# TensorE's two programs change places behind its branch, three long plain float32 products stand in front of the branch, and TensorE's last wait goes

## What is computed

```
gate = x W_gate^T + 0.5 * B_gate[i] (A_gate[i] x)      # i: the entry's own low-rank weights, 16 to choose from
up   = x W_up^T   + 0.5 * B_up[i]   (A_up[i] x)
act  = silu(gate) * up
down = act W_down^T + 0.5 * B_down[i] (A_down[i] act)
m    = max(max|down|, 1e-5) per token
out  = x + (down / m) W_2bit^T * (m * scale) + bias    # W_2bit: four levels, -1.5 to 1.5
```

## Time and profile before

| | us |
|---|---|
| median of 3 runs | 896.11 (895.1 to 896.49) |
| the profiled execution | 895.7 |
| its span in the profile | 894.0 |
| TensorE busy | 877.1 (98% of the span) |
| VectorE, ScalarE, GpSimd busy | 414.6, 275.3, 82.3 |

### The profile page before, as it was taken

How to read it: one execution, slowest core, us unless ns; L and a number is a source line. 1 busy time by engine, 2 the same in 40 slices (tenths; PEclk the granted TensorE clock), 3 DMA queues, 4 the chain that set the end, 5 groups by cost and what they waited for, 6 DMA issues and landing times.

```text
span 894.0 us, 12944 instructions
## 1 busy us (share of the span) xinstructions
PE 877.1 (98%) x3880; PEld 710.1 (79%) x3880; DVE 414.6 (46%) x813; ACT 275.3 (31%) x518; POOL 82.3 (9%) x117
## 2 busy tenths in 40 slices
PE   6999999999999999999999999999999999999996
PEld 6788788888888888888888888888888888878875
DVE  4653467333572236623464234832258223573334
ACT  3642442223421224222333114322242223412113
POOL 1100012010030000300003000030001200020110
PEclk9999999999999999999999999999999999999999
DMA  5532222110201011110111101111111110010011
GB/s 176 150 116 75 91 61 58 49 27 18 63 26 48 23 26 56 38 36 23 38 44 38 36 23 52 39 42 31 28 52 41 39 32 15 14 36 23 23 36 50
DMA packets 43834, 42.33 MB, mean 47 GB/s; under 512 B 12656, under 2 KB 30832, under 8 KB 43808
## 3 DMA queue, kind: packets, MB, share of 16 engines
q1 hardware_dynamic: 41904, 39.16, 15.8%
q10 hardware_dynamic: 1744, 2.56, 0.9%
q0 software_dynamic: 160, 0.33, 0.1%
HBM read 33.62 MB, written 8.39 MB: 47 GB/s over the span
## 4 chain that ended last, share of the span: by engine, by line
PE 94%; DMA 2%; DVE 1%; ACT 1%; issue 1%; SPq 0%; DVEq 0%; ACTq 0%
PE pp_up L1939 26%; PE pp_gate L1939 24%; PE pp_down L2017 23%; PE ps_misc L2073 6%; PE ps_td L2006 4%; PE ps_misc L1939 2%; PE pp_down L2027 2%; PE pp_up L1986 2%; PE pp_gate L1986 2%; DMA rows<-w_gu 2%; PE pp_gate L1929 1%; PE pp_down L2073 1%; ACT wgu L895 0%; DVE actp_full L1551 0%; PE pp_down L2042 0%
## 5 line engine op out<-in xcount | busy, mean ns | idle before, releaser
L2017 PE MATMUL pp_down<-actp_split,wd 128*128 128x512 f32 x960 | 233.3, 392 | 0.0
L1939 PE MATMUL pp_up<-xw,wgu 128*128 128x512 f32 x948 | 229.4, 391 | 0.3 <-DVE actp_full L1551 0.3
L2017 PEld LDWEIGHTS pp_down<-actp_split,wd 128*128 128x128 f32 x960 | 180.3, 188 | 45.1
L1939 PEld LDWEIGHTS pp_up<-xw,wgu 128*128 128x128 f32 x948 | 178.3, 188 | 39.1 <-DVE actp_full L1551 0.7
L1939 PE MATMUL pp_gate<-xw,wgu 128*128 128x512 f32 x864 | 208.0, 390 | 0.9 <-ACT actp_full L1079 0.8
L1551 DVE TENSOR_TENSOR actp_full<-pp_up,actp_full 128x512 f32<-128x512 f32 (+1 forms) x87 | 60.1, 690 | 299.6 <-PE pp_up L1986 278.0
L1939 PEld LDWEIGHTS pp_gate<-xw,wgu 128*128 128x128 f32 x864 | 162.0, 188 | 35.7 <-issue 1.7
L1079 ACT ACTIVATE actp_full<-pp_gate 128x512 f32<-128x512 f32 (+1 forms) x80 | 47.6, 595 | 288.6 <-PE pp_gate L1986 288.6
L1095 ACT ACTIVATE actp_split<-actp_full 128x512 fp32r<-128x512 f32 x80 | 50.6, 632 | 161.4 <-DVE actp_full L1551 157.6
L1047 ACT ACTIVATE bp_split<-b_raw 32x256 fp32r<-32x256 f32 (+1 forms) x176 | 71.2, 405 | 2.4
L1560 DVE TENSOR_TENSOR actp_split<-actp_full,actp_split 128x512 fp32r<-128x512 f32 x80 | 55.4, 692 | 21.2 <-ACT actp_split L1095 20.9
(11 more groups left out here) (135 smaller groups left out, 646.1 us busy)
## 6 DMA issues: line engine op xcount, KB each, us to landing
x_raw<-x_feat SPq DMA_DIRECT2D x118, 64.0 KB, 1.7
rows<-w_gu SPq DMA_DIRECT2D x8, 512.0 KB, 4.4
rows<-x_tok SPq DMA_DIRECT2D x64, 64.0 KB, 1.8
more_rows<-x_tok SPq DMA_DIRECT2D x64, 64.0 KB, 1.8
out<-rows SPq DMA_DIRECT2D x64, 64.0 KB, 1.6
out<-more_rows SPq DMA_DIRECT2D x60, 64.0 KB, 1.6
rows<-w_down SPq DMA_DIRECT2D x9, 256.0 KB, 2.6
b_raw<-b_rows SPq DMA_DIRECT2D x16, 92.0 KB, 2.5
```

The costliest lines, as they stand in the source:

```text
L1939: return nc.tensor.matmul(ps_out[0:m, a:b], w, xw[:, part, k, a:b], start=start, stop=stop)
L2017: last = nc.tensor.matmul(pp_down[:, h, :], wd[0:w, wp, f, h * P:(h + 1) * P], actp_split[0:w, ap, f % 2, :], start=(f == 1 and n == 0), s ...
```

## The change

TensorE alone gets new instructions. Its branch is turned round: "if the flag is 0: general program, else: pair program", so that the general program stands right behind the branch and the pair program behind that one, in front of the end of the block. The flag is loaded ahead of `ps_run` instead of behind it. Between `ps_run` and the branch stand three new products of 128x512 on plain float32 operands (the same bytes as the warm-up's, read as float32). The warm-up has 11 products ahead of the flag where it had 10, and 2 at the head of the pair program where it had 24. The wait for `stored_rows[2]` at the end of the pair program is gone. The other engines run as before.

```diff
-WARM_UP = (10, 24)
+WARM_UP = (11, 2)
+LONG_WARM_UP = 3
...
-                pe.wait_ge(stored_rows[2], 16 * 4 * WIDE_TILES)
-
             pe.wait_ge(columns_ready, 2)
             pe.wait_ge(one_hot_ready, 1)
             nc.tensor.matmul(ps_plan, plan_columns, one_hot, start=True, stop=True).then_inc(plan_gathered, 1)
             warm_up(0)
+            flag = pair_flag(pe)
             pe.wait_ge(run_column_ready, 1)
             nc.tensor.matmul(ps_run, run_column, one_hot, start=True, stop=True).then_inc(run_gathered, 1)
-            flag = pair_flag(pe)
-            with pe.If(flag == 1):
+
+            for _ in range(LONG_WARM_UP):
+                nc.tensor.matmul(pp_gate[:, :], wgu_chunk(HI, 1)[:, 0, 0, :].bitcast(F32),
+                                 wgu[:, HI, 0:WIDE].bitcast(F32), start=True, stop=True)
+            with pe.If(flag == 0):
+                general_program()
+            with pe.Else():
                 pair_program()
-            with pe.Else():
-                general_program()
```

## The result

The changed kernel is slower: 896.93 us as a median of 11 runs (895.97 to 898.39) against 895.64 for the kernel before in 11 runs beside them (894.65 to 896.81). The ratio is 1.0020 with a 95% interval of 1.0013 to 1.0028, some 1.8 us. The forecast was 894.7, a small gain or none. The time lies above the range. One of the 11 executions of the change with its wait kept took 1263.64 us; it is left out of the ratio, and without it the median of 896.96 in the table would be 896.84.

What follows compares the result with a forecast made beforehand. TensorE was taken to bound the kernel (94% of the chain). Gains of 1.1 us at the start and 0.3 at the end took 895.7 to 894.3 for the profiled execution, 894.7 as median; range 893.7 to 896.6.

Steps and rivals of the forecast that it cites:

- The branch, the jump and the long products: Start of TensorE: the taken jump costs 2.9 to 3.8 us, covered by three four-pass products of 1.82 us each.
- the third rival: Start: short long products and a long jump leave TensorE idle 2.6 us or more at low clock; 898.0 us, chance 0.10.
- the clock's rise: TensorE's start: the clock goes from 1.2 to 2.4 GHz at 12.8, after 5.75 us of unbroken row from 7.02.
- The step that failed: Start: new fetches among x's and the weights' loads, one of 16 engines held 1.3 us, cut the 1.3 gain to 1.1.
- the low part of x at 14.10: Start: the first half's first low part, ready at 14.10 as before, lets products on x begin at 14.2, not 15.75.
- The first rival: Start: TensorE's fetches push x's loads by 1.3 us and take back the gain; end's 0.3 left, 895.7 us, chance 0.24.
- The end: End of the kernel: without TensorE's fetch ScalarE's and SyncE's jumps may shorten; gain 0 to 0.6 us, taken as 0.3.
- The sum: Whole kernel: 895.7 - 1.1 (start) - 0.3 (end) = 894.3 us for the profiled execution; median 896.1 - 1.4 = 894.7.

Runs made afterwards that it cites:

- the jump behind chunk 1: The change with TensorE's pair program in two parts, warm-up, first chunk and chunk 1 right behind a first branch, the rest behind the general program: 894.12 us, 0.9984.
- the pair program first: The change with the programs in the old order, pair program right behind the branch, and TensorE's last wait back: 894.11 us, ratio 0.9992 to the kernel before.
- three engines divided: TensorE's pair program in two parts as with the jump behind chunk 1, and ScalarE's and SyncE's divided too: 892.94 us, ratio 0.9973 to the kernel before.

## Why the prediction was wrong

**The branch, the jump and the long products: right in kind.** The jump was put at 2.9 to 3.8 us and took 4.49 here, 4.0 to 6.4 in others at the start, which is longer than the range; the long products were put at four passes, 1.82 each, and hid it. Where all of them ran at the low clock, with the jump behind chunk 1, the chain has:

```profile
10.57 5.42 PE pp_gate L2159 x6
```

Six records are three products, two each: 1.81 us a product. The Trainium skill's four passes for true float32 ("FP8 and Floating Point Precision", section "TensorE Precision Notes") agree with this. No gap stands on TensorE while it jumps, and the third rival (short products and a long jump) did not come about.

Two smaller terms were wrong here. `ps_run` was to follow the warm-up at once, at no cost; in this execution TensorE waited 0.58 us for VectorE in front of it, since the flag and all that hangs on it came late. In two executions with an earlier flag (8.67 and 8.69) there is no such wait. And the clock's rise was put at 12.8, carried over from the kernel before by the length of the unbroken row. The trace's record of full clock begins at 14.33 in the change. It begins at 12.43 with the pair program first, where the row had a gap of 0.33 at 9.8, and at 13.41 and 13.44 in two kernels whose row had none, so it can't be carried over in that way. Neither cost anything in the change, since x's first half was later still; with x in time the rise decides how much the start gains (below).

**The step that failed: "The new fetches fall among x's loads and the weights' (one packet holds one of 16 engines 1.3 us), so I count 1.1"**. With it went the low part of x at 14.10, which the sum took over from the kernel before. With the old order and no fetch at the start, chunk 1 came 1.20 us earlier behind the flag than before, where 1.1 to 1.3 had been worked out. That so much came is in part luck with the clock, whose record there begins at 12.43: with the jump behind chunk 1 the gain was 0.39 (record from 15.89), and 1.03 with three engines divided (from 14.66). With the fetches the two halves came 1.46 and 3.16 us later, and chunk 1 came 2.18 later (1.49 and 2.12 in the other two executions of this start). I took 0.2 us off for it; against the kernel with the pair program first it was worth 2.7 to 3.4.

The first rival had the mechanism, "TensorE's fetch, and the next one behind it, push the x loads", but let it only take back the gain. It moved the second half by one packet's 1.3 us. The first half moved as well, so ScalarE, whose issue of the second half's last loads stands behind its first split, issued late; and the second packet fell among those. The reason given against it, that one engine of 16 is held, was wrong: the split waits for the last sixteenth, so holding one part of 16 is enough. That the jump makes x late is shown by moving it, later in three kernels and away in one, with x's loads as they were: the splits return to 4.11 to 4.48 and 7.52 to 7.78 (before: 4.24 and 7.85). That it does so through one sixteenth of each load is shown by the counts of landings: three late ones on three queues in the change, the last of them 1.70 us behind the 94th, and no gap over 0.24 us in front of the last count in the kernels without a jump there. The trace doesn't name the engine of a packet; that the late sixteenths sit on the packet's engine is inferred from their number and time. The packet itself lasts 0.96 us in the change, less than the 1.46 by which the first half is late: what waits behind it still has to move (eight packets of ScalarE's queue, a sixteenth of a load, moved from 14.08 to 14.27, the first of that queue since 12.65). How the rest divides stays open.

The Trainium skill warned of the stall of the engine that jumps ("Runtime: NRT & Kernel Launch", section "Instruction fetch mechanics"). The stall is in the trace, 4.49 us, and was paid for by queued work; the loss was x's.

**The end: right in kind, too small.** The forecast's 0.3 was 0.8 on the average, 1.1 in the profiled execution. Its reason, that TensorE's packet lay among the others' transfers, stands: taking away the wait alone left a packet there and gained nothing, taking away the jump alone gained as much as both, and the last stores end about a microsecond earlier without it.

**The sum.** For the profiled execution the start loses 2.18 + 0.53 by the late flag, the end gives 1.1, and 0.7 of the lateness is made up on the way to the last block (2.71 at chunk 1, 1.98 there), which makes 0.9 in the span (894.9 against 894.0). Without the late flag, which is chance, it would be 0.4; the medians say 1.3, the ratio 1.8. Single executions differ by a microsecond, as the table's rows do among themselves, and the sizes here are no better than that.

## What to carry to other kernels

A taken jump has two prices: the stall of its engine, which queued work can cover, and the packets that it fetches, which can hold up what is being loaded at that time (here the last sixteenth of three loads). Put the jump where neither the engine nor the loads are late (here behind chunk 1, or in the steady part), and keep what runs at the start and what runs at the end in a row with the branch. When an engine is freed, look at what is late next and ask whether the change itself disturbs that.

## What the runs showed of the hardware that was not expected

- While a packet of TensorE's instructions moved among x's loads (0.96 us), 94 of 96 sixteenths of these loads landed by 13.06 and the last one 1.70 us later.
- A taken jump over TensorE's other program took 3.64 us at 23.2, 4.49 at 10.2 and 6.40 at 17.3; what loads ran meanwhile differed.
- The three long products took 3.89, 4.80 and 5.49 us in three kernels with the same warm-up ahead of them (first of their rows at 10.30, 10.36 and 10.50). The record of full clock begins at 12.43, 14.33 and 15.89 there, so the low clock lasted through all of them in the last one only. What decides when the clock rises these runs don't show.
- ScalarE's drain behind VectorE's last block fell from 3.6 us (TensorE alone in two parts) to 1.1 once its program ended in a row with the barrier: 2.5 us of it had been the jump.
